# One graph network layer's edge pass, with a second job laid into it

## The chip, the cores and the metric

The program runs on one core of one Trainium2 chip. Its time is the device time of one execution in microseconds. The five engines that appear here are PE (TensorE, matrix products; its weight loads are listed apart as PEld), DVE (VectorE), ACT (ScalarE), POOL (GpSimd, which here issues the indirect DMAs that gather rows) and SP (SyncE, which issues the plain DMAs). Each engine has one queue and works it off in order. They meet only through semaphores.

## The reference, cut to what matters

Four graph layers follow one another over the same graph of 6250 nodes and 100,000 edges, each with a residual and a layer norm. The edges are sorted by their target `dst`, and the targets are dense at the start: `dst = 6250 * u**2`.

```python
edge_index = stack([src, dst])
x = layernorm(x + L0(x, node_vec1, src, dst, edge_attr_4, edge_attr_10, ...))
x = layernorm(x + L1(x, edge_index, ...))   # gated messages, GRU
x = layernorm(x + L2(x, edge_index, ...))   # two sort convolutions
x = layernorm(x + L3(x, edge_index, ...))   # four mean aggregations (SAGE)

def L0(...):                                # the tensor layer
    h = silu(edge_attr_10 @ W_fc1 / sqrt(10))      # edges x 100
    w = h @ W_fc2 / sqrt(100)                      # edges x 128
    x0s, x1s = y0[src], y1[src]                    # y = a linear map of the node's x
    ... = products of w, x0s, x1s and edge_attr_4
    agg = segment_sum(edge_features, dst)          # edges to 256 sums a node
def sage(z):                                # in L3
    mean = segment_sum(z[src], dst) / max(count, 1)
    return mean @ Wl.T + bl + z @ Wr.T
```

## The kernel before

**Edges and tiles.** A tile is 128 edges, one a partition; a group is four tiles; there are 196 groups. Nodes are columns: the 6250 nodes lie in 49 blocks of 128. Five regions of SBUF of 6400 columns (`X` and `A` to `E`, in the rows `x` and `ra` to `re`) hold node features and spare room.

**Two ways to sum over edges.** For a cold group POOL gathers the source rows of its edges by four indirect DMAs, and PE multiplies them with a one-hot matrix of the targets. For the first, hot part of the sorted edges, where many edges share few targets, the kernel builds once a count matrix: how many edges run from each source node to each of a range of target nodes. It lies in HBM as `dense`, in 16 bits, and the gate pass and the four SAGE passes read it back block by block and multiply it with the whole table of source rows; edges that it covers are not gathered there. The tensor layer (L0) has features of each edge's own and so gathers all 784 tiles.

**The count matrix.** Its target columns are cut in windows of `NARROW` = 32 nodes; a window takes as many whole tiles as fall into 27 expected nodes, 16 at most (`hot_cuts`, L51). For every tile DVE makes two one-hots, of the low seven bits of the source (128 wide, L1418) and of block and target together (49 x 32 = 1568 wide, L1419), PE multiplies them into PSUM (L1434), and ACT copies a finished window into a stage of eight windows (L1448), which SP stores to `dense`. 64 windows (380 tiles) are built in `build_phase`, which runs by itself before anything else of the network; the other 64 (148 tiles) are built inside the two sort phases of L2 by `LateBuild` (L2298, L2303, L2316, L2328), one tile at a turn between the sort's own instructions. The gate pass uses 2048 columns of it, the wide SAGE passes 2304, the slim ones 4096.

**The order of the phases.** Preparation of indices; build; scaling of weights; `table_phase`, which writes the table of `y` (L283, L299, L311); `tensor_pass`; its closing products; table, gate pass and GRU of L1; two sorts; then for each of the four SAGE layers a table, a pass and statistics. A phase is a block: all engines leave it before the next begins.

**The tensor pass** (L905 on) has for each group, by engine:
- POOL: four gathers (L953) into a ring of four groups of rows.
- SP: the next 10 x 512 edge inputs.
- PE: the hidden layer of the group after next as an f32 product over 10 rows (L996), the weights of the next group (four products, L1005), then 8 products with the one-hot of the targets (L1025, L1027).
- ACT: SiLU of the hidden layer (L970), four scaled copies of the gathered rows (L983).
- DVE: the one-hot of the targets (L1050), eight products and sums of the features (L852 to L864), two additions into the node regions (L1043).
The body is written once for four groups and looped 49 times. PE and DVE are one or two groups apart, held by semaphores; POOL may be four groups ahead.

**A SAGE pass** (`sage_pass`) lays 98 dense steps (49 blocks for each of two halves of the columns, three 16-bit terms of the table each, L1611) between its cold groups (products L1637), with the layer's own product (L1593). All steps lie in the cold groups but the last seven (wide) or five (slim). When a half is summed ACT copies it out of PSUM (L1568), DVE multiplies every window by its nodes' inverse counts (L1712) and adds it (L1720).

## Time and profile before

| | us |
|---|---|
| runs | 4872.65, 4879.16, 4879.4 |
| median | 4879.16 |
| the profiled execution | 4866.0 |
| its span on the core | 4863.8 |
| granted TensorE clock, mean | 0.873 |

The rows come from that one profiled execution. In it the preparation ends at 23.9 us, the build at 296, the first gather of the tensor pass starts at 325.2 and its last sums are added at 1358.5; the gate pass runs from 1448 to 2030, the sorts from 2175 to 2740, and the four SAGE passes from 2816, 3306, 3888 and 4450, of 364, 484, 483 and 347 us. A row of the stretches gives for each engine its busy time and in brackets its instructions. Busy times of PE are unions in which the tail of each product is modelled, so what a product costs is read from the distance of two starts. A row of a group of instructions gives count, busy time, mean duration in ns and the idle time before, with what ended it. Idle time of an engine that is not the bound costs nothing.

### The profile page before, as it was taken

How to read it: one execution, taken by the hardware profiler on the slowest of the kernel's cores; microseconds unless marked ns; L12 is line 12 of the kernel's file. 1: busy time of each engine (PE TensorE's matmuls, PEld its weight loads, DVE VectorE, ACT ScalarE, POOL GpSimd, SP SyncE). 2: the span in 40 equal slices, each digit the busy share in tenths (PEclk: the TensorE clock that was granted, in tenths of full speed). 3: DMA queues.
4: the chain of work that ended last, by engine and by line, in shares of the span. 5: the costliest groups of instructions: out<-in, count | busy, mean ns of one | idle time of the engine just before them, and what ended most of it. 6: DMA issues, size and time to landing. Idle time of an engine off the chain costs nothing. (4 is left out here: it accounts for less than half of the span.)

```text
span 4863.8 us, 78847 instructions
## 1 busy us (share of the span) xinstructions
PE 3902.5 (80%) x25115; PEld 2612.6 (54%) x25167; DVE 2854.8 (59%) x8895; ACT 1285.8 (26%) x2773; POOL 3033.0 (62%) x3029
## 2 busy tenths in 40 slices
PE   8978989888987777656645579968999599986995
PEld 3446667666664454433322345546767477664553
DVE  8966666666646767567768724263343634444234
ACT  1343333333324434343333400021011201012112
POOL 0037777777727767547757666727777477774764
PEclk9989898898889989876556789989999799997996
DMA  2352222222224434212243387818888388875873
GB/s 79 91 170 55 54 54 55 54 54 54 54 73 101 109 91 108 65 36 78 76 117 103 110 262 238 248 50 259 264 255 251 111 269 265 258 217 184 269 243 107
DMA packets 434350, 679.63 MB, mean 140 GB/s; under 512 B 66928, under 2 KB 297370, under 8 KB 433270
## 3 DMA queue, kind: packets, MB, share of 16 engines
q1 hardware_dynamic: 310774, 373.35, 24.5%
q0 software_dynamic: 123264, 302.38, 22.5%
q8 instruction: 164, 2.69, 0.2%
q14 instruction: 148, 1.21, 0.1%
HBM read 575.89 MB, written 99.58 MB: 139 GB/s over the span
## 5 line engine op out<-in xcount | busy, mean ns | idle before, releaser
L1541 POOL DMA_INDIRECT pass_rows<-table_sage,src_idx x1264 | 1231.0, 974 | 456.5 <-issue 368.4
L953 POOL DMA_INDIRECT pass_rows<-table_tensor,src_idx x784 | 783.3, 999 | 257.6 <-issue 236.8
L1672 DVE TENSOR_TENSOR pass_scaled_sums<-pass_sums_ps,rc 128x128 f32<-128x128 f32 x508 | 130.1, 287 | 955.4 <-PE pass_sums_ps L1637 949.8
L1611 PE MATMUL pass_dense_ps<-x 128*128 128x512 f16 (+3 forms) x3528 | 607.0, 327 | 31.8 <-DMA x<-table_sage 31.0
L1611 PE MATMUL pass_dense_ps<-rb 128*128 128x512 f16 x2352 | 535.2, 383 | 28.2 <-DMA rb<-table_sage 26.7
L1153 POOL DMA_INDIRECT pass_rows<-table_gate,src_idx x402 | 423.5, 1053 | 192.4 <-issue 116.4
L2375 POOL DMA_INDIRECT sort_rows<-table_sort,slot_idx x392 | 391.2, 998 | 183.1 <-issue 117.3
L1637 PE MATMUL pass_sums_ps<-pass_hot,pass_rows 128*128 128x128 bf16 x6096 | 412.0, 225 | 76.1 <-issue 74.4
L1611 PEld LDWEIGHTS pass_dense_ps<-x 128*128 128x128 bf16 x3528 | 314.4, 98 | 266.4 <-DMA x<-table_sage 32.4
L1025 PE MATMUL pass_sums_ps<-pass_hot,pass_prod_a 128*128 128x128 f32 x1568 | 363.1, 319 | 111.1 <-DVE pass_prod_b L852 110.9
L1637 PEld LDWEIGHTS pass_sums_ps<-pass_hot,pass_rows 128*128 128x128 bf16 x6096 | 383.6, 101 | 101.5 <-issue 83.1
L983 ACT ACTIVATE pass_y_ea<-pass_rows,rd 128x128 f32<-128x128 f32 x784 | 250.2, 390 | 507.1 <-DMA pass_rows<-table_tensor,src_idx 507.0
L1611 PEld LDWEIGHTS pass_dense_ps<-rb 128*128 128x128 bf16 x2352 | 226.9, 99 | 285.3 <-DMA rb<-table_sage 29.0
L1025 PEld LDWEIGHTS pass_sums_ps<-pass_hot,pass_prod_a 128*128 128x128 f32 x1568 | 284.0, 226 | 130.4 <-issue 129.8
L1027 PE MATMUL pass_sums_ps<-pass_hot,pass_prod_b 128*128 128x128 f32 x1568 | 354.0, 313 | 0.0
L2316 PE MATMUL sort_counts_ps<-sort_hot_key,sort_hot_low 128*128 128x512 bf16 (+1 forms) x571 | 193.2, 483 | 179.5 <-DVE sort_hot_key L2303 137.7
L1005 PEld LDWEIGHTS pass_weight_ps<-fc,pass_hidden 100*128 100x128 f32 x1576 | 201.2, 200 | 165.8 <-issue 162.7
L1238 PE MATMUL pass_dense_ps<-pass_weighted,rd 128*128 128x512 f32 x392 | 206.4, 651 | 102.2 <-DVE pass_weighted L1317 102.2
L1027 PEld LDWEIGHTS pass_sums_ps<-pass_hot,pass_prod_b 128*128 128x128 f32 x1568 | 287.8, 229 | 0.0
L1434 PE MATMUL build_counts_ps<-build_hot_key,build_hot_low 128*128 128x512 bf16 (+1 forms) x1490 | 266.4, 330 | 4.9 <-DVE build_hot_key L1419 2.6
L852 DVE TENSOR_TENSOR pass_y_ea<-pass_rows,rd 128x384 f32<-128x384 f32 x196 | 110.7, 565 | 240.4 <-DMA pass_rows<-table_tensor,src_idx 240.4
L996 PE MATMUL pass_hidden_ps<-pass_edge_in,fc 10*100 10x512 f32 x396 | 235.2, 675 | 18.3 <-DMA pass_edge_in<-in_edge_in 18.3
(331 smaller groups left out, 6758.6 us busy)
## 6 DMA issues: line engine op xcount, KB each, us to landing
rb<-dense SPq DMA_DIRECT2D x196, 512.0 KB, 3.8
x<-dense SPq DMA_DIRECT2D x196, 288.0 KB, 3.8
x<-table_sage SPq DMA_DIRECT2D x196, 192.0 KB, 4.7
pass_counts<-dense SPq DMA_DIRECT2D x98, 256.0 KB, 3.0
dense<-re SPq DMA_DIRECT2D x7, 3136.0 KB, 12.8
pass_rows<-table_sage,src_idx POOLq DMA_INDIRECT x1264
rb<-table_sage SPq DMA_DIRECT2D x196, 96.0 KB, 5.2
table_sage<-x SPq DMA_DIRECT2D x24, 768.0 KB, 3.5
```

What stands on the lines that cost most here:

```text
L953: nc.gpsimd.indirect_dma_start(rows[:, h, t, :], None, table, bass.IndirectOffsetOnAxis(ap=idx[:, at:at + 1], axis=0)).then_inc(gathered[h ...
L983: ins = nc.scalar.activation(y_ea0[:, r, t, :], rows[:, h, t, :], ACT.Copy, scale=cols(extra["edge_attr"], (q * GROUP_TILES + t) * 4, 1))
L996: nc.tensor.matmul(hidden_ps[0:HID, r4 % 2, :], extra["w_fc1"], edge_in[:, r4, :], start=True, stop=True).then_inc(hidden_summed, 1)
L1025: nc.tensor.matmul(sums[0][:, r, 0:WIN], prod_a[:, r, t, :], hot[:, r, t, :], start=first, stop=last)
L1027: ins = nc.tensor.matmul(sums[1][:, r, 0:WIN], prod_b[:, r, t, :], hot[:, r, t, :], start=first, stop=last)
L1153: nc.gpsimd.indirect_dma_start(rows[:, h, t, :], None, table, bass.IndirectOffsetOnAxis(ap=idx[:, at:at + 1], axis=0)).then_inc(gathered[h ...
L1238: ins = nc.tensor.matmul(dense_ps[:, at:at + 512], messages[:, k, 0:P], weighted[:, n % 2, at:at + 512], start=(b == 0), stop=(b == BLOCKS ...
L1434: ins = nc.tensor.matmul(counts[:, w % 2, at:at + wide], hot_low[:, r, :], hot_key[:, r, at:at + wide], start=(t == first), stop=(t == last))
L1541: nc.gpsimd.indirect_dma_start(rows[:, h, t, :], None, table, bass.IndirectOffsetOnAxis(ap=idx[:, at:at + 1], axis=0)).then_inc(gathered[h ...
L1611: ins = nc.tensor.matmul(dense_ps[:, at:to], table_ring[:, k, from_table:from_table + P], counts_ring[:, k, at - first:to - first], start= ...
L1637: ins = nc.tensor.matmul(sums[:, r, a * P:(a + 1) * P], rows[:, h, t, at:at + P], hot[:, r, t, :], start=(t == 0 and part == 0), stop=(t = ...
L2375: nc.gpsimd.indirect_dma_start(rows[:, b, j, :], None, table, bass.IndirectOffsetOnAxis(ap=slot_idx[:, at:at + 1], axis=0)).then_inc(gathe ...
```

## The change

**The build moves.** `build_phase` is gone. `tensor_pass` makes a `LateBuild` for the first 376 tiles and gives its turns to the first 190 of its 196 groups, two tiles a turn nearly everywhere: DVE makes the one-hots behind the group's own one-hot, PE multiplies behind the hidden layer, ACT copies a finished window behind its four row copies, and SP stores a finished stage. There is one stage (`E`), one PSUM accumulator for the window, and three buffers for the wide one-hot. The last SP work of the pass is the load of the node attributes, which before came ahead of the pass.

**The pass is written out.** All 49 turns of the loop are now separate code, on every engine.

**The first layer.** The 10 edge inputs and the 10 x 100 weights are each split in three bf16 terms; all nine pairs are stacked to 90 rows and one bf16 product (L1172 of the new program) takes the place of the f32 one. The edge inputs' terms are made in `first_table_phase`, eight chunks of 990 columns (ACT copy, DVE difference, POOL cast and DVE difference, then a store of 742 KB), beside the table; each store waits until the one before has landed. The pass reads them back in rounds of four groups, by three DMAs. The weights' terms are made in `split_weights` and go through HBM.

**Loads.** Weights, `x`, five of the eight chunks of edge inputs and the edge attributes are issued behind the preparation's own loads.

**The windows.** `hot_windows` chooses cuts and a width of its own for each window (at most 30 nodes wanted, some widened to 32) so that the widths just fill 1792, 2304 and 3840 columns. The gate pass reads 1792 columns (before 2048) for 376 tiles (380); the wide passes 2304 (2304) for 420 (404); the slim ones 3840 (4096) for 536 (528). With 784 tiles in all, cold groups are 102 (101), 91 (95) and 62 (64). A tile of the first 376 has 1232 key columns in the mean, at most 1470 (before 1568 each); in 41 of 68 places one window ends and the next begins in the same turn. The sorts build 160 tiles (148) of 1310 columns in the mean (1568).

**SAGE sums.** DVE copies the inverse counts of a half's windows side by side (`spread_counts`) and evacuates the half out of PSUM itself by one multiplication (`keep_dense`), so that a window then needs one addition. Before that ACT evacuated and DVE multiplied window by window.

```diff
@@ tensor_pass
-        sums = [s.ps(f"sums{a}", [P, 2, 512]) for a in range(A)]
+        sums = s.ps("sums", [P, 2, 512])
+        edge_terms = s.sb("edge_terms", [STACK, 2, ROUND_COLS], BF16)
+        build = LateBuild(nc, s, *extra["build"])
@@ sync
+            sp.wait_ge(extra["split_stored"], 16 * SPLIT)
+            stages = list(range(len(build.runs)))
+            for i in range(ITERS + 1):
+                if i >= 2:
+                    sp.wait_ge(hidden_summed, RING * (i - 1))
+                if i >= 1:
+                    sp.wait_ge(terms_loaded, 16 * PARTS * i)
...
+                for q in list(stages):
+                    if build.stage_turn(q, BUILD_TURNS) < RING * (i - 1):
+                        build.store(sp, stages.pop(0))
...
+            extra["attributes"].issue(sp)
@@ scalar, behind the four row copies
+                    for t in build.turns(q, BUILD_TURNS):
+                        for w in build.ended(t):
+                            build.evict(act, w)
-            looped(act, ITERS, body)
+            for i in range(ITERS):
+                body(i)
@@ tensor
-                nc.tensor.matmul(hidden_ps[0:HID, r4 % 2, :], extra["w_fc1"], edge_in[:, r4, :],
+                nc.tensor.matmul(hidden_ps[0:HID, :], extra["w_terms"],
+                                 edge_terms[:, q // RING % 2, q % RING * 512:(q % RING + 1) * 512],
...
-                    hidden_layer(i + (1 if h + LOOK >= 4 else 0), q + LOOK, r4)
                     weights(q + 1, (h + 1) % 2)
+                    hidden_layer(q + LOOK)
+                    for t in build.turns(q, BUILD_TURNS):
+                        build.products(pe, t)
@@ vector, behind the one-hot of the targets
+                for t in build.turns(q, BUILD_TURNS):
+                    build.one_hots(dve, t)
@@ LateBuild.evict
+        if w == first and stored > 0:
+            act.wait_ge(self.stored[q % n], 16 * stored)
+        act.wait_ge(self.counted, HOT_CUTS[w + 1] - self.start)
@@ sage_pass
-            def keep_dense(u):
-                if u > 0:
-                    act.wait_ge(dense_added, u * super_windows * A)
-                act.wait_ge(stepped, (u + 1) * BLOCKS)
-                nc.scalar.activation(kept, dense_ps[:, 0:sage_cols], ACT.Copy).then_inc(dense_kept, 1)
+            def keep_dense(u):
+                if u > 0:
+                    dve.wait_ge(dense_added, parts_of[u][0][0] * A)
+                dve.wait_ge(spread, sum(map(len, parts_of[:u + 1])))
+                dve.wait_ge(stepped, (u + 1) * BLOCKS)
+                for a in range(A):
+                    at = a * super_cols
+                    nc.vector.tensor_tensor(kept[:, at:at + super_cols], dense_ps[:, at:at + super_cols],
+                                            inv_dense[:, 0:super_cols], ALU.mult).then_inc(dense_kept, 1)
@@ gnn_kernel
-                build_phase(nc, "build", key, low, late_key[:], late_low[:], wide_iota, dense, [C, E], dense_stored,
-                            [first, attributes])
-            table_phase(nc, "tab0", [X], t0, ident, rhs=[wl1[:]], row_scale=attr_col, clear=[A[:], B[:]])
-            node_attributes.start_after(dense_stored, 16 * (GATE_WINDOWS // STAGE_WINDOWS))
+            first_table_phase(nc, X, t0, wl1[:], attr_col, [A[:], B[:]], [terms_out, terms_in], flat_edges, left, parts, flat_terms,
+                              edges_loaded, split_stored)
```

**The order on DVE** in the tensor pass, one group (turn) of the new program from one one-hot of the targets to the next. `rc` is room in region `C`: the 512 wide row makes the low one-hots of four tiles (every other turn), the x2 row the key one-hots of two tiles, here of windows 12 nodes wide.

```order
L1225 TENSOR_TENSOR pass_hot<-iota,rel 128x512 [waits prep_counted]
L2441 TENSOR_TENSOR rc<-rc 128x512 [waits pass0_counted]
L2447 TENSOR_SCALAR rc<-rc 128x588 [waits pass0_counted] x2
L1015 TENSOR_TENSOR pass_y_ea<-pass_rows,rd 128x384 [waits prep_step,gathered2]
L1015 TENSOR_TENSOR pass_w_y<-pass_weight_ps,pass_rows 128x128 [waits pass0_weight_made]
L1024 TENSOR_TENSOR pass_dot<-pass_y_ea 128x4x32 [waits pass0_step]
```

Before, the row after the one-hot of the targets was the product with the gathered rows; now three one-hot instructions of the build stand between them.

**The order on PE**, one group of the tensor pass, of the program before from one hidden layer to the next:

```order
L996 MATMUL pass_hidden_ps<-pass_edge_in,fc 100x512 [waits pass0_edge_in_loaded3,pass0_hidden_made]
L1003 REGISTER_ALU [waits prep_step]
L1005 MATMUL pass_weight_ps<-fc,pass_hidden 128x128 [waits pass0_hidden_made]
L1005 MATMUL pass_weight_ps<-fc,pass_hidden 128x128 x3
L1021 REGISTER_ALU
L1025 MATMUL pass_sums_ps<-pass_hot,pass_prod_a 128x128 [waits prep_step,prep_turned]
```

and the same stretch of the new one:

```order
L1182 MATMUL pass_weight_ps<-fc,pass_hidden 128x128 [waits pass0_hidden_made,prep_step]
L1182 MATMUL pass_weight_ps<-fc,pass_hidden 128x128 x3
L1172 MATMUL pass_hidden_ps<-pass_edge_terms,fc_stack 100x512 [waits pass0_hidden_made]
L2461 MATMUL pass_counts_ps<-rc 128x512 [waits pass0_key_made,pass0_low_made]
L2461 MATMUL pass_counts_ps<-rc 128x76
L2461 MATMUL pass_counts_ps<-rc 128x512 [waits pass0_key_made,pass0_low_made]
L2461 MATMUL pass_counts_ps<-rc 128x76
L1203 MATMUL pass_sums_ps<-pass_hot,pass_prod_a 128x128 [waits prep_step,prep_turned]
```

The hidden layer went behind the weights, and the products of two tiles of the count matrix stand ahead of the group's sums.

**The order on ACT** in the new tensor pass, around the end of a stage. `re` is the stage in region `E`:

```order
L2479 ACTIVATE re<-pass_counts_ps 128x49x26 [waits pass0_counted]
L1141 ACTIVATE pass_hidden<-pass_hidden_ps 100x512 [waits pass0_hidden_summed,pass0_weight_made]
L1154 ACTIVATE pass_y_ea<-pass_rows,rd 128x128 [waits gathered2,prep_step]
L1154 ACTIVATE pass_y_ea<-pass_rows,rd 128x128 x3
L2479 ACTIVATE re<-pass_counts_ps 128x49x20 [waits pass0_counted,dense_stored]
L1141 ACTIVATE pass_hidden<-pass_hidden_ps 100x512 [waits pass0_hidden_summed,pass0_weight_made]
```

Here the copies of windows stand between the SiLU and row copies of the groups, and the first copy of a new stage waits until the store of the one before has landed.

## Rows read from the trace of the kernel before

**Rows 1.** Stretches: us, busy (count) by engine; clock, DMA share, GB/s.

```profile
23.90:296.40 272.50, 266.39 (x1490) 119.70 (x1520) 266.92 (x762) 95.77 (x65) 0.00 (x0) 1.00 0.34 103
296.40:325.20 28.80, 15.51 (x98) 15.13 (x98) 8.72 (x14) 7.31 (x8) 10.80 (x2) 0.75 0.81 235
325.20:1358.50 1033.30, 911.55 (x5108) 697.09 (x5108) 704.16 (x2155) 357.68 (x982) 783.28 (x784) 0.87 0.22 57
...
2816.00:3180.00 364.00, 335.12 (x2195) 195.08 (x2194) 122.57 (x445) 21.53 (x51) 253.64 (x254) 0.96 0.79 245
3306.00:3790.00 484.00, 462.62 (x4364) 331.72 (x4364) 201.75 (x781) 46.69 (x100) 364.68 (x378) 0.98 0.82 255
...
4450.00:4797.00 347.00, 324.42 (x2093) 184.09 (x2094) 114.77 (x393) 45.72 (x99) 247.76 (x254) 0.96 0.81 249
```

**Rows 2.** DVE in order of time, in the build: start, duration, instruction.

```profile
149.98 0.62 DVE L1419 TENSOR_SCALAR build_hot_key<-wide_iota,key 128x1568 bf16<-128x1568 f16 x1
150.52 0.25 DVE L1418 TENSOR_SCALAR build_hot_low<-wide_iota,low 128x128 bf16<-128x128 f16 x1
```

**Rows 3.** Gathers on POOL: count, busy us, mean ns, idle before and its releasers.

```profile
L953 POOL DMA_INDIRECT pass_rows<-table_tensor,src_idx x784 | 783.3, 999 | 257.6 <-issue 236.8 <-POOLq L153 16.5 <-PE pass_sums_ps L1027 4.4
L1153 POOL DMA_INDIRECT pass_rows<-table_gate,src_idx x402 | 423.5, 1053 | 192.4 <-issue 116.4 <-POOLq L153 39.2 <-PE pass_sums_ps L1266 36.7
L2375 POOL DMA_INDIRECT sort_rows<-table_sort,slot_idx x392 | 391.2, 998 | 183.1 <-issue 117.3 <-POOLq L153 64.3 <-DVE sort_t L2444 1.5
```

**Rows 4.** One line's durations (ns min/median/max), first and last start.

```profile
L953 POOL DMA_INDIRECT pass_rows<-table_tensor,src_idx x784: 940/944/1536, 325.2 to 1348.8; - x196
```

**Rows 5.** DVE in order of time, one group of the tensor pass.

```profile
906.85 0.69 DVE L1050 TENSOR_TENSOR pass_hot<-iota,rel 128x512 f32<-128x512 f32 x1
908.55 0.56 DVE L852 TENSOR_TENSOR pass_y_ea<-pass_rows,rd 128x384 f32<-128x384 f32 x1 [1.01 <-DMA pass_rows<-table_tensor,src_idx]
...
909.90 0.29 DVE L852 TENSOR_TENSOR pass_prod_a<-pass_weight_ps,pass_y_ea 128x128 f32<-128x128 f32 x1 [0.40 <-ACT pass_y_ea L983]
...
911.84 0.69 DVE L1050 TENSOR_TENSOR pass_hot<-iota,rel 128x512 f32<-128x512 f32 x1
```

**Rows 6.** PE in order of time, tensor pass, at both clock levels.

```profile
907.88 0.39 PE L1027 MATMUL pass_sums_ps<-pass_hot,pass_prod_b 128*128 128x128 f32 x2
908.10 0.39 PE L1025 MATMUL pass_sums_ps<-pass_hot,pass_prod_a 128*128 128x128 f32 x2
...
908.64 1.10 PE L996 MATMUL pass_hidden_ps<-pass_edge_in,fc 10*100 10x512 f32 x2
909.67 1.16 PE L1005 MATMUL pass_weight_ps<-fc,pass_hidden 100*128 100x128 f32 x8
...
912.66 0.64 PE L1025 MATMUL pass_sums_ps<-pass_hot,pass_prod_a 128*128 128x128 f32 x2
913.09 0.63 PE L1027 MATMUL pass_sums_ps<-pass_hot,pass_prod_b 128*128 128x128 f32 x2
```

**Rows 7.** The wide one-hot inside the sort phases.

```profile
L2303 DVE TENSOR_SCALAR sort_hot_key<-keys_iota,late_key 128x1568 bf16<-128x1568 f16 x148 | 94.3, 637 | 0.0
```

**Rows 8.** Table phases: a PSUM evacuation on DVE, a cast on POOL.

```profile
L299 DVE TENSOR_TENSOR tab_rows<-tab_turned_ps,attr_col 128x896 f32<-128x896 f32 x7 | 7.6, 1092 | 14.4 <-DMA table_tensor<-tab_rows 7.6 <-PE tab_turned_ps L283 6.7
...
L351 POOL CAST x<-tab_rest 128x1024 bf16<-128x1024 f32 (+1 forms) x26 | 46.3, 1781 | 152.7 <-DVE tab_rest L400 152.5
```

**Rows 9.** DMA issues: count, KB each, median us from issue to landing.

```profile
dense<-re SPq DMA_DIRECT2D x7, 3136.0 KB, 12.8
...
table_sage<-x SPq DMA_DIRECT2D x24, 768.0 KB, 3.5
```

**Rows 10.** PE in order of time in a wide SAGE pass.

```profile
3450.25 1.50 PE L1637 MATMUL pass_sums_ps<-pass_hot,pass_rows 128*128 128x128 bf16 x24
3451.59 3.09 PE L1611 MATMUL pass_dense_ps<-x 128*128 128x512 f16 x18
3454.52 1.06 PE L1593 MATMUL pass_own_ps<-pass_z_block,sage_wr 128*128 128x128 f32 x8
```

610 lines of the change are left out of this document (374 added, 236 removed).

## The prediction

> **What bounds the kernel now.** I read the stretches first, to find the phases in which the change puts or takes work. From 23.9 to 296.4 us the build runs with DVE busy 267 of 272.5 us and PE 266, and POOL not at all [rows 1]. From 325.2 to 1358.5 the tensor pass has PE busy for 912 of 1033 us at a granted clock of 0.87, and DVE for only 704 [rows 1]. In the build, one key one-hot starts 0.54 us ahead of what follows it, though its duration is given as 0.62 [rows 2]: instructions overlap at their ends, so I cost DVE by distances of starts. Then the gathers: 784 of them have a mean of 999 ns and 236.8 us of "issue" between them, 0.302 us each, so 1.30 us for one and 5.2 us for a group of four; waits for PE are 4.4 us in all [rows 3]. First and last start are 325.2 and 1348.8, 1.307 us apart in the mean [rows 4]. POOL thus never rests: it sets the length of this pass. The group of DVE agrees. From one target one-hot to the next 4.99 us pass, and in them DVE is idle for 1.01 us until a gather lands and for 0.40 us until ACT has scaled the rows [rows 5]. It occupies 3.58 us of a group and leaves 1.4 to 1.6. On PE two starts of product pairs are 0.22 us apart at the full level (2.4 GHz) and 0.43 us at the lower one (1.2 GHz) [rows 6]. Eight pairs (1.78), the hidden layer (1.03, the distance to the next instruction) and the weights (about 1.0) make 3.8 us a group at the full level. A mean clock of 0.87 is 26% of the time at the lower level.
>
> **The tensor pass with the build in it.** A turn gets 376 / 190 = 1.98 tiles. DVE: a key one-hot has 1232 columns in the mean against 1568, between 0.42 us (in proportion to the 0.54) and 0.54; I take 0.45, since part of it does not shrink. The low one-hots of four tiles are one 512 wide instruction like the target one-hot, about 0.6, so 0.15 a tile. 1.98 x 0.60 = 1.2 us, and DVE is at 4.8 us of a group. That is less than POOL's 5.2, with 0.4 us to spare: the cover is thin but it is there. The added instructions stand where DVE now idles for the gather. PE loses the f32 hidden layer (1.03) and gets one product of 512 columns (0.22) and 1.98 x 1232 columns at 2.4 a ns (1.03): 4.0 us a group at full level. ACT has 358 us of work in the pass and gets 69 window copies of some 1.2 us; its time is no bound. Its place in the row matters: where one window ends and the next begins in one turn (41 times) PE waits about 1.5 us for the copy; PE has 1.2 us to spare a turn and the next turn makes up the rest, so I put it at nothing. Behind the wait for a stored stage ACT's SiLU and row copies queue, and PE and DVE behind these. A store lands 12.8 us after its issue, about 2.4 turns; the next stage's first window ends one to three turns after the old stage's last. So ACT is held for up to 8 us, at six places. POOL may be 16 gathers (21 us) ahead and DVE wins back 0.4 us a turn, with some 15 to 30 turns between the later stages: nothing in the sum, 48 us if none is made up.
>
> What isn't free is POOL against DVE. The median gather takes 944 ns, the mean 999 [rows 4, 3]: 55 ns each are lost already, in groups without a key one-hot. In the sort phases, where 148 key one-hots run beside 392 gathers, the mean is 998 [rows 7, 3], so the keys add nothing that can be told from the rest. If all the excess there (392 x 54 ns = 21 us) were the keys', one would cost 0.14 us. For 376 keys that bounds the price by 0 and 54 us; I take the middle, **+27 us**.
>
> The Trainium skill speaks against this part: "SBUF — State Buffer", section "Who interferes with whom", says that DVE in a two-port mode (16-bit `tensor_scalar` is of that kind) shuts GpSimd out of the shared port for the whole instruction, descriptor writing included. If every key one-hot did that, it would be the port rival below; the sort phases' mean of 998 ns does not bear it out.
>
> **The start.** The build goes with all its time; what it covered comes out. Its block covered the loads of `x` and the edge attributes, which now run behind the preparation's: `x` and five chunks of edge inputs are 5.6 MB, at the pace of a stage store (3136 KB in 12.8 us [rows 9]) 23 us after about 10, so 33 at the latest. The preparation is longer by two or three DVE instructions and a DMA (1.4 us by my estimate), then four key copies, waits and the scaling with the split of the weights (5 us). The table phase begins near 30 (26 to 34). The first chunk needs the ACT copy, DVE difference, POOL cast and DVE difference one after another behind a table evacuation. A DVE pass over 896 columns takes 1.09, a cast of 1024 on POOL 1.78 [rows 8]: 990 columns are about 1.2 and 1.7, and the first store is issued near 41. Then seven more. DVE has 1.09 + 2 x 1.2 = 3.5 us of work for each, and a store must land before the next is issued: one of 768 KB lands in 3.5 us [rows 9], with issue and handover 4.2. I take 4.2 (3.5 if DVE alone is the bound, 6.5 if table stores and reloads halve the pace). 41 + 7 x 4.2 = 70, and three block changes make 73 for the first gather (62 to 92), where it is at 325.2 now. **-252 us** (-263 to -233). That the first sums must wait until the terms are back, some 8 us, POOL's lead covers.
>
> **The other passes.** Gate: a step of 896 columns instead of 1024 is shorter by about 0.1 us on ACT and DVE and 0.2 on PE, 98 times, but only the 36.7 us in which POOL waits for PE [rows 3] can be won; one cold group more costs 4 x 1.4. **-3 us** (-15 to +8). Sorts: 160 tiles of 1310 columns for 148 of 1568, at the same POOL pace: nothing (+-4). Wide SAGE: a step is 2.93 us, the sums of a group 1.34, the own product of a block about 0.9 [rows 10]. While the steps last PE has 98 x 2.93 + 49 x 0.9 + 88 x 1.34 = 449 us against POOL's 88 x 4 x 1.25 = 440: both are full. The last seven groups are POOL's, 36 us. Sum 485, measured 484. Now there are 86 groups with steps and 5 without: 446 + 25.5 = 472. -13 each. Slim SAGE: PE is busy 335 of 364 and 324 of 347 us [rows 1]; a step loses 128 columns of three products, 0.16 us, 98 times, and eight tiles go with 24 products: 17 us if PE were the bound throughout, I take -14 each. Against that PE waits at each half for two multiplications of DVE (about 1.3 us each) behind whatever DVE is at, where it was one free ACT copy: +2 a pass (0 to +5). Together **-46 us** (-60 to -22).
>
> **The sum.** The profiled execution took 4866.0 us. -252 + 27 - 3 - 46 = -274 gives 4592. The median of the runs is 13.2 us above the profiled execution, and I carry that over: **4605 us**.
>
> **The rivals.**
> *DVE and ACT become the bound of the pass.* For it: DVE's 0.4 us a group. If the wait of 0.40 us for ACT stays and the one-hots cost their full durations (0.62 and 0.17), a turn is 3.58 + 0.40 + 1.98 x 0.79 = 5.54 against POOL's 5.33 with the contention of the sum: +40, and with 48 us of held ACT 4693. Against it: the waits are there because the gathers are late, and go when DVE is.
> *The port.* Each key one-hot stops a gather for its own 0.49 us (0.45 to 0.54): 376 x 0.49 = 184, 157 more than in the sum, 4762. Against it the 998 ns.
> *The saving is taken up by PE at the lower level: slower than before.* In place of the POOL bound PE bounds every turn. At 1.2 GHz a turn is 8.0 us, the pass 1568 us, 523 more than in the sum, 5130. For it: single accumulator waits break PE's work up, and PE is at the lower level 26% of the time now. It cancels the gain from a group of 6.7 us, 4.0 x (1 + s), so a share s of 0.68. Against it: a turn has more columns and less idle time than now, and the clock is 1.00 in the build, where PE is never idle [rows 1]. The skill's "TensorE: Matmul & The Clock Gate", section "What's actually happening", has it that activity releases the throttle, which would raise the clock here; the 0.87 and 1.00 agree.
> *The side gains don't come:* SAGE bound by its DMAs and chunks at 6.5 us: +46 and +16, 4667.
> *Better:* no contention, stage and table at their lower ends, 4550.
>
> **How the numbers follow.** Forecast 0.56 (4570 to 4640), DVE and ACT 0.18, port 0.05, lower level 0.02, side gains missing 0.12, better 0.07. The range leaves out the port, the lower level and the outer end of the others: 4545 to 4700. A measurement of this kernel can tell about 0.2% from no change; all cases but the lower level are faster by more. Faster 0.97, same 0.01, slower 0.02.
>
> **What would show it.** First gather at 62 to 92 us; a distance between gathers of 1.31 to 1.38 us over the pass with a mean near 1030 ns; POOL's waits for PE there still under 20 us; DVE busy near 90% and its wait for gathers much smaller; clock above 0.87; wide passes near 471, slim ones near 350 and 333. The forecast is wrong if gathers wait for PE's sums for tens of us, if many gathers last 1.4 us or more, or if the gate pass and the sorts move by over 10 us.

## The result, and the profile after

The changed kernel takes **4712.9 us** (median of four, 4711.0 to 4720.1) against 4879.3 for the kernel before (four, 4872.7 to 4879.7): a ratio of 0.9663, 95% interval 0.9649 to 0.9677. It is faster by 166 us, not by the 274 of the forecast (4605), and lies 13 us outside the range. The profiled execution took 4711.4 us, so between the two profiled executions the gain is 154.6 us (4866.0 less 4711.4), 120 less than the 274 of the sum. Between medians only 108 are missing. The 12 us between these two numbers are luck: the forecast carried over the 13.2 us by which the median stood above the profiled execution, and now that distance is 1.5.

The profile after, in stretches (us, then busy us and count by engine PE, PEld, DVE, ACT, POOL; clock, DMA share, GB/s): the first table phase, the tensor pass, the gate pass's two halves, the first slim SAGE pass, what follows it, a wide and the last slim pass.

```profile
30.00:94.80 64.80, 20.35 (x98) 19.10 (x98) 25.71 (x23) 16.14 (x17) 25.02 (x16) 0.63 0.52 165
94.80:1172.00 1077.20, 850.70 (x5879) 692.66 (x5880) 915.76 (x2598) 430.00 (x1041) 834.37 (x784) 0.93 0.33 90
1273.00:1576.00 303.00, 225.05 (x1281) 155.02 (x1281) 189.56 (x547) 118.23 (x296) 227.08 (x212) 0.89 0.39 99
1591.00:1870.00 279.00, 202.00 (x1160) 133.50 (x1157) 190.33 (x568) 113.93 (x294) 206.60 (x194) 0.93 0.38 94
2665.00:3025.00 360.00, 321.45 (x2156) 192.75 (x2156) 127.83 (x491) 17.62 (x48) 240.19 (x246) 0.94 0.76 237
3025.00:3166.00 141.00, 78.78 (x310) 56.05 (x310) 82.30 (x184) 31.81 (x44) 33.68 (x40) 0.78 0.19 70
3166.00:3630.00 464.00, 449.72 (x4236) 320.44 (x4236) 195.18 (x731) 42.44 (x97) 348.18 (x362) 0.99 0.82 258
4285.00:4630.00 345.00, 309.15 (x2060) 181.87 (x2060) 120.21 (x446) 41.62 (x96) 237.41 (x246) 0.95 0.77 239
```

Beside [rows 1]: the build's 272 us are gone; the tensor pass is 1077 us where it was 1024, at a clock of 0.93 for 0.87, with DVE at 85% and PE less busy than before; wide passes went from 482 to 463 us; slim ones stayed where they were (360 and 344 to 345) although they have 8 gathers less and 256 columns less.

The table sets the distances between gathers against the forecast, in us, all from profiled executions. The last column is e17, the best kernel of this study, explained below.

| stretch | before | after | change | forecast | e17 |
|---|---|---|---|---|---|
| to the first gather of the tensor pass | 325.2 | 94.8 | -230.4 | -252 | 81.1 |
| tensor pass, first gather to end of last | 1024.5 | 1076.9 | +52.4 | +27 | 1075.7 |
| to the gate pass's first gather | 98.8 | 101.4 | +2.6 | 0 | 103.2 |
| gate pass | 576.6 | 596.4 | +19.8 | -3 | 564.6 |
| to the end of the second sort | 705.5 | 712.1 | +6.5 | 0 | 706.8 |
| to the first SAGE gather | 85.5 | 83.9 | -1.6 | 0 | 83.9 |
| slim SAGE passes (two) | 703.9 | 703.6 | -0.3 | -24 | 674.2 |
| wide SAGE passes (two) | 962.0 | 927.1 | -34.8 | -22 | 925.2 |
| between and after the SAGE passes | 381.9 | 413.4 | +31.5 | 0 | 349.8 |

The gathers answer to [rows 3] (busy us, mean ns, idle before them and what ended it):

```profile
L1124 POOL DMA_INDIRECT pass_rows<-table_tensor,src_idx x784 | 834.4, 1064 | 246.8 <-issue 236.8 <-PE pass_sums_ps L1203 5.7 <-POOLq L201 4.3
L1333 POOL DMA_INDIRECT pass_rows<-table_gate,src_idx x406 | 433.7, 1068 | 202.3 <-issue 118.2 <-PE pass_sums_ps L1452 44.5 <-POOLq L201 39.6
```

POOL still sets the pass: 236.8 us of issue as before and 5.7 us of waits for PE. A gather is 65 ns longer, and 784 x 65 ns = 51 us is the whole of the pass's +52. So the missing 120 us are: the start 22, the contention of this pass 25, the gate pass with the gap ahead of it 25, the sorts with the gap ahead of them 7, and SAGE 41, most of that between the passes and not in them.

**What the queues show.** The stretches that follow a slim pass are longer by 11 us each, and PE waits there for DVE (once for 13.0 us). DVE's row in order of time, at the end of the last pass (in brackets its idle time before and what ended it):

```profile
4628.16 7.49 DVE L1847 TENSOR_TENSOR ra<-ra,pass_kept 128x32 f32 x24 [5.20 <-issue]
...
4642.50 7.45 DVE L1847 TENSOR_TENSOR ra<-ra,pass_kept 128x24 f32 x24 [5.18 <-issue]
```

and at the start of the same pass, with the same number of windows:

```profile
4305.13 2.81 DVE L1821 COPY pass_inv_dense<-rc 128x28 f32 x24 [1.41 <-issue]
```

5.2 us of "issue" against 1.4 ahead of 24 windows. What stands there is the load of 24 window starts into registers. It is listed on the sequencer (DVEq, PEldq), with the least, median and longest duration in ns, then first and last start. Before:

```profile
L1123 DVEq TENSOR_LOAD <-bases x50: 309/355/979, 1475.4 to 2041.9; - x50
L1123 PEldq TENSOR_LOAD <-bases x26: 306/336/348, 1458.5 to 2033.1; - x26
...
L1646 DVEq TENSOR_LOAD <-hot_bases x40: 818/1104/1415, 2993.3 to 4813.5; - x40
```

After:

```profile
L1303 DVEq TENSOR_LOAD <-bases x51: 315/961/982, 1300.4 to 1889.0; - x51
L1303 PEldq TENSOR_LOAD <-bases x26: 530/1004/1026, 1284.4 to 1871.5; - x26
...
L1760 DVEq TENSOR_LOAD <-hot_bases x64: 310/1604/5383, 2686.4 to 4665.7; - x64
```

Put beside the first table entry that each load asks for (worked out from the window and group counts of both kernels), the loads of these passes fall into two rows, PE and DVE within 0.1 us of each other; only the first load of the first slim pass stands out, with 3.3 us:

```
values loaded                       4      6      8     12     16     24
first entry a multiple of 4      0.34   0.82   0.60   0.85   1.10   1.60 us
any other first entry            0.97   1.41   1.85   2.73      -   5.37 us
```

The change moved first entries. The second half of a slim pass began at window 64 and begins at 73; of a wide one at 36, now 45; the starts of the gate pass's cold groups were read from entry 96 on, now from 95. (The kernel before had such loads too: sixes from entries that are no multiple of 4 in its wide passes, 1.41 us, and fours in the gate and SAGE passes, 0.97.)

### The profile page after: what moved, and what is told of

It reads as the page before. It is cut to its first block and busy times, and to the rows that moved or that the text cites. A ratio compares the mean times of both kernels' runs of the same rounds, so it can differ in the third digit from the quotient of the medians.

```text
span 4709.5 us, 73302 instructions
## 1 busy us (share of the span) xinstructions
PE 3546.9 (75%) x24179; PEld 2502.4 (53%) x24180; DVE 2819.4 (60%) x8637; ACT 1252.7 (27%) x2796; POOL 3057.2 (65%) x2999
## 5 line engine op out<-in xcount | busy, mean ns | idle before, releaser
L1664 POOL DMA_INDIRECT pass_rows<-table_sage,src_idx x1216 | 1175.8, 967 | 476.7 <-issue 350.3
L1124 POOL DMA_INDIRECT pass_rows<-table_tensor,src_idx x784 | 834.4, 1064 | 246.8 <-issue 236.8
L1725 PE MATMUL pass_dense_ps<-rb 128*128 128x512 f16 (+1 forms) x2352 | 508.7, 373 | 27.4 <-DMA rb<-table_sage 25.2
L2461 PE MATMUL sort_counts_ps<-sort_hot_key,sort_hot_low 128*128 128x512 bf16 (+4 forms) x502 | 190.8, 519 | 194.2 <-DVE sort_hot_key L2447 150.5
L1203 PE MATMUL pass_sums_ps<-pass_hot,pass_prod_a 128*128 128x128 f32 x1568 | 234.9, 297 | 131.8 <-DVE pass_prod_b L1015 131.0
L1203 PEld LDWEIGHTS pass_sums_ps<-pass_hot,pass_prod_a 128*128 128x128 f32 x1568 | 209.7, 206 | 186.7 <-issue 177.8
L2461 PE MATMUL pass_counts_ps<-rc 128*128 128x512 bf16 (+8 forms) x1039 | 238.1, 355 | 88.5 <-ACT re L2479 88.5
L1424 PE MATMUL pass_dense_ps<-pass_weighted,rd 128*128 128x512 f32 (+1 forms) x392 | 191.8, 616 | 113.2 <-DVE pass_weighted L1503 110.7
L1203 PE MATMUL pass_sums_ps<-pass_hot,pass_prod_b 128*128 128x128 f32 x1568 | 228.9, 294 | 0.0
L1182 PE MATMUL pass_weight_ps<-fc,pass_hidden 100*128 100x128 f32 x1576 | 221.5, 286 | 1.5 <-ACT pass_hidden L1141 1.0
L1203 PEld LDWEIGHTS pass_sums_ps<-pass_hot,pass_prod_b 128*128 128x128 f32 x1568 | 212.8, 211 | 0.0
```

What stands on the lines that cost most here:

```text
L1124: nc.gpsimd.indirect_dma_start(rows[:, h, t, :], None, table, bass.IndirectOffsetOnAxis(ap=idx[:, at:at + 1], axis=0)).then_inc(gathered[h ...
L1182: ins = nc.tensor.matmul(weight_ps[:, r, t * P:(t + 1) * P], hidden[:, r, t * P:(t + 1) * P], extra["w_fc2"], start=True, stop=True)
L1203: ins = nc.tensor.matmul(sums[:, r, a * WIN:(a + 1) * WIN], prod[:, r, t, :], hot[:, r, t, :], start=(t == 0), stop=(t == GROUP_TILES - 1))
L1424: ins = nc.tensor.matmul(dense_ps[:, at:to], messages[:, k, 0:P], weighted[:, n % 2, at:to], start=(b == 0), stop=(b == BLOCKS - 1))
L1664: nc.gpsimd.indirect_dma_start(rows[:, h, t, :], None, table, bass.IndirectOffsetOnAxis(ap=idx[:, at:at + 1], axis=0)).then_inc(gathered[h ...
L1725: ins = nc.tensor.matmul(dense_ps[:, at:to], table_ring[:, k, from_table:from_table + P], counts_ring[:, k, at - first:to - first], start= ...
```

## The experiments

The register loads, the split's order on DVE, the one-hots and the transfers were each tried alone. e5 to e16 form a second group: there the kernel before takes 5498 to 5500 us and not 4878 to 4881 as beside the others. The record numbers the chips 12, 14 and 1 in this group and 13 and 14 in the first, so the number of the chip does not tell them apart; what does is not known. What is compared in the second group is compared with runs of that group. There is no result of e4, in which each key one-hot was to be written twice.

**e1: register loads from a multiple of four.** In both `load_bases` of the gate and SAGE passes:

```diff
+lead = at % 4
-source[0:1, at:at + count]
+source[0:1, at - lead:at + count]
-return values
+return values[lead:]
```

> The changed kernel, with one edit: each batched load of window starts into registers (gate pass on TensorE and VectorE, SAGE passes on VectorE) begins at a table entry whose number is a multiple of 4, with up to three entries more than are used. Theory A: in the changed kernel such a load costs about 0.22 us for each value when it begins elsewhere (24 values 5.37 us, 12 values 2.73 us, 8 values 1.85 to 1.93 us, 4 values 0.96 to 1.0 us), and 1.60, 0.85, 0.60 and 0.34 us when it begins at a multiple of 4; the change moved the second half's windows from 64 or 36 to 73 and 45, and the gate pass's cold groups from 95 to 94, off such entries. Then the loads of 24 fall to about 1.8 us, the gate pass (596 us from first to last gather) gets 10 to 18 us shorter, its gap between the halves 4 us, each slim SAGE pass and its tail 15 to 22 us, each wide one 5 to 8 us: 55 to 85 us in all, about 4630 to 4660 us. Theory B: the loads lie beside waits, and the passes are longer because the adds of 24 windows are one chain: then the loads get shorter but the time falls by less than 15 us, to no less than 4698 us.

Measured: 4653.0 us, ratio 0.9536 (0.9512 to 0.9559), 60 us off. Its profiled execution was its fastest, 4636.5, so its stretches add up to 75 us of gain where the medians have 60. The slim passes took 347.2 and 331.5 us (360 and 344), what follows the first slim one 131.0 (141.2), the tail 69.9 (80.3); wide passes with their gaps were 7.0 and 8.6 us shorter; the gap between the gate's halves was 11.1 us for 16.2. DVE ahead of the same 24 windows:

```profile
4570.89 7.43 DVE L1849 TENSOR_TENSOR ra<-ra,pass_kept 128x24 f32 x24 [1.67 <-issue]
```

Theory A. With this alone the slim passes are 13 and 12 us below those of before, which is the forecast's term. Only the gate pass was short of it, 9 us of 10 to 18 (587.5 us; in four profiles with the loads as they were, of after, e2, e3 and e18, it took 595.0 to 609.0, so these 9 are hardly more than the scatter). The expectation names entries 95 and 94; they are 96 and 95, and 94 and 95 are both no multiples of 4, so nothing else in it changes. On PE a load was no faster than before the edit, since 4 values had become 7.

```profile
L1304 PEldq TENSOR_LOAD <-bases x26: 593/1064/1082, 1284.6 to 1858.5; - x26
```

**e2: the third term ahead of the next remainder.** In the first table phase on DVE:

```diff
+                if 0 <= i - 1 < SPLIT:
+                    third_term(i - 1)
                 if i < SPLIT:
                     take_first(i)
-                if 0 <= i - 1 < SPLIT:
-                    third_term(i - 1)
```

> The changed kernel, with two calls exchanged on VectorE in the first table phase: the third term of chunk i-1 is made before the first remainder of chunk i. Theory A: a chunk takes 8 us there, not 4.2, because the store of chunk i-1 stands behind the remainder of chunk i, which waits for ScalarE's copy, which waits for the landing of the store of chunk i-2: landing (4.5 us), copy, remainder and third term in one chain. With the exchange the store of chunk i-1 no longer waits for that landing, the pace falls to 5 to 6 us a chunk, and the first gather of the tensor pass moves from 94.8 to 72 to 82 us; the time falls by as much, to 4690 to 4700 us. Theory B: the pace is set by the stores themselves (landing after landing, with the table's store and a reload between them on the same queue), and stays at 7 to 8 us; the first gather stays within 5 us of 94.8.

Measured: 4700.6 us, ratio 0.9623 (0.9600 to 0.9647), 12 us off; first gather at 80.3, 14.5 us sooner. The profiled execution was the slowest of its four, 4713.2, with a gate pass of 609.0 us; no edit touches that pass. One chunk in after, from the landing of a store (ACT's copy, then DVE's remainder, then its third term of the chunk before) to the next store's issue:

```profile
45.69 1.03 ACT L393 ACTIVATE re<-re 128x990 bf16<-128x990 f32 x1 [8.94 <-DMA edge_terms<-re]
...
46.75 1.19 DVE L430 TENSOR_TENSOR re<-re 128x990 f32<-128x990 f32 x1 [4.54 <-ACT re L393]
...
47.86 1.18 DVE L435 TENSOR_TENSOR re<-re 128x990 bf16<-128x990 f32 x1
48.01 1.90 POOL L383 CAST re<-re 128x990 bf16<-128x990 f32 x1 [4.55 <-DVE re L430]
49.07 0.36 SPq L460 DMA_DIRECT2D edge_terms<-re  x1
```

and issues of stores in order of time, after:

```profile
41.24 0.38 SPq L460 DMA_DIRECT2D edge_terms<-re  x1
...
49.07 0.36 SPq L460 DMA_DIRECT2D edge_terms<-re  x1
...
57.16 0.36 SPq L460 DMA_DIRECT2D edge_terms<-re  x1
```

and in e2:

```profile
52.23 0.36 SPq L460 DMA_DIRECT2D edge_terms<-re  x1
...
58.00 0.36 SPq L460 DMA_DIRECT2D edge_terms<-re  x1
...
63.79 0.36 SPq L460 DMA_DIRECT2D edge_terms<-re  x1
```

8.0 us a chunk became 5.8: theory A. A store lands 4.2 us after its issue (median; 3.8 in e2), and in after 3.4 us of copy, remainder and third term follow before the next one. The exchange also parted POOL's casts from DVE's third term; of after and of e2 (busy us, mean ns, idle before):

```profile
L383 POOL CAST re<-re 128x990 bf16<-128x990 f32 x6 | 10.3, 1718 | 55.2 <-DVE re L430 55.2
```

```profile
L383 POOL CAST re<-re 128x990 bf16<-128x990 f32 x6 | 6.1, 1010 | 51.0 <-DVE re L430 51.0
```

The first mean mixes durations: of all eight casts six run beside a third term (L435) from nearly their start to its end and take 1.90 us, one takes 1.70 and one 1.01; in e2 none overlaps a third term and all take 1.01.

**e3, e18: the one-hots of the build left out.** Key one-hots 8 columns wide after the first three tiles (e3), and the low ones 8 of 128 too after two groups (e18):

```diff
+some = keys
+if self.start == 0:
+    some = BUILD_KEYS if t < self.RINGS else 8
-self.nc.vector.tensor_scalar(self.hot_key[:, r, 0:keys], self.iota[:, 0:keys], ...
+self.nc.vector.tensor_scalar(self.hot_key[:, r, 0:some], self.iota[:, 0:some], ...
```

> The changed kernel, where the wide key one-hots of the tensor pass's build are written for the first three tiles only and 8 columns wide after that, so that the matrix of counts is wrong; products, evictions, stores and all waits stay. Theory A: a gather takes 1064 ns in the tensor pass instead of 999 because VectorE's 16-bit key one-hots (376 of 561 ns) hold up GpSimd; without them the mean is 995 to 1010 ns, and the pass from first to last gather takes 1020 to 1035 us instead of 1077. Theory B: the gathers are held up by the added transfers (the stacked terms three times over, the seven stores of the matrix): the mean stays above 1045 ns and the pass above 1060 us.

> The kernel of e16_no_hots (key and low one-hots of the tensor pass's build 8 columns wide; the matrix of counts is wrong), which beside the unaltered one took 28 ns off the mean gather, and e14_no_low_hots 10 ns, where the gathers had waits of their own. Where they have none, e3_no_key_hots took off 38 ns of 65. Theory A (the rest is the low one-hots and scales as the key one-hots do): another 12 to 25 ns, a mean of 1001 to 1014 ns and a pass of 1025 to 1042 us. Theory B (the rest is not the one-hots'): 1018 to 1026 ns and 1044 to 1050 us.

Measured, in e3 and in e18 (one execution of each):

```profile
L1124 POOL DMA_INDIRECT pass_rows<-table_tensor,src_idx x784 | 804.4, 1026 | 249.7 <-issue 235.9 <-PE pass_sums_ps L1203 9.5 <-POOLq L201 4.3
```

```profile
L1124 POOL DMA_INDIRECT pass_rows<-table_tensor,src_idx x784 | 783.9, 1000 | 255.5 <-issue 236.5 <-PE pass_sums_ps L1203 14.8 <-POOLq L201 4.2
```

The mean goes 1064, 1026, 1000, and before it was 999 [rows 3]; the pass 1077, 1050, 1035 us. So e3 fell between its theories, and e18 confirms the first: the one-hots are all of it. The key ones cost 38 ns a gather, 30 us in all or 0.08 us for each of 376; the low ones 26 ns, 20 us or 0.22 us for each of 94. The last 10 us between 1035 and the 1024.5 of before are POOL's waits for the sums, 14.8 us against 4.4. The added transfers are all there in e18, whose gather is as long as before: they have no part in the mean.

**e7, e11, e14, e16, e8, e12: the same question in the second group.** e7, e11 and e16 are e18's kernel, e14 has the low one-hots alone 8 wide, e8 and e12 (one kernel) load the stacked terms in full for two rounds only, and 8 columns after that:

```diff
+wide = wide if i < 2 else 8
```

> As e3_no_key_hots, and the low one-hots of the tensor pass's build are written 8 columns wide too after the first two groups (the matrix of counts is wrong). e3_no_key_hots took the mean gather from 1064 to 1026 ns, not to 999. Theory A: the other 27 ns are VectorE's as well, the low one-hots (94 of 681 ns) and the small instructions: the mean falls to 1000 to 1015 ns. Theory B: they are the added transfers: the mean stays at 1020 to 1030 ns.

> The changed kernel where the stacked edge terms are loaded in full for the first two rounds of the tensor pass only, and 8 columns wide for the other 47 (the first layer's result is wrong). Theory A: added transfers are part of what lengthens the gathers: the mean falls from 1064 to 1040 to 1050 ns and the pass from 1077 to 1055 to 1065 us. Theory B (VectorE alone): the mean stays at 1058 to 1068 ns, the pass within 5 us of 1077.

> The kernel of e7_no_hots again (key and low one-hots of the tensor pass's build written 8 columns wide; the matrix of counts is wrong), for a look beside e3_no_key_hots where the gathers have no other waits. In e7_no_hots the mean gather fell from 1041 (e5_whole_fours there) to 1004 ns. Theory A (VectorE's one-hots are the whole of it): 995 to 1012 ns, and the pass 1022 to 1038 us. Theory B (the low one-hots have no part): 1020 to 1030 ns as in e3_no_key_hots, and the pass 1045 to 1055 us.

> The kernel of e8_less_traffic again (the stacked terms in full for two rounds of the tensor pass only; the first layer's result is wrong), for a look where the gathers have no other waits. In e8_less_traffic the mean was 1044 ns beside 1041 in e5_whole_fours. Theory A (transfers have a part): mean 1040 to 1050 ns, pass 1055 to 1065 us. Theory B: mean 1058 to 1068 ns, pass 1072 to 1082 us.

> The changed kernel with only the low one-hots of the tensor pass's build written 8 columns wide after the first two groups (94 instructions of 681 ns become short; the matrix of counts is wrong). e3_no_key_hots took 38 of the 65 ns that a gather gained. Theory A (the other 27 ns are the low one-hots): the mean falls by 20 to 30 ns against e13_changed_again, the pass by 15 to 22 us. Theory B (they come from the instructions' number and what shifts against what, not from these): by less than 10 ns and 8 us.

> The kernel of e7_no_hots and e11_no_hots beside the unaltered one: key and low one-hots both 8 columns wide (the matrix of counts is wrong). Theory A (VectorE's one-hots are the whole of what a gather gained): its mean is 55 to 65 ns under e13_changed_again's where nothing else holds the gathers, and the pass 45 to 55 us shorter; where the gathers wait for remote, 30 to 40 ns and 10 us or less. Theory B (27 ns are not theirs): 35 to 42 ns and 25 to 32 us.

Mean gather there: 1032 ns in the changed kernel (e13), 1033 to 1041 in five others with all one-hots, 1004, 1010 and 1005 without any, 1023 without the low ones, 1044 and 1034 with fewer transfers. Transfers have no part that shows; the low one-hots have some 10 ns, the key ones some 18. The pass lengths say little: 1220 to 1234 us without one-hots and 1248 in e13, but 1231 to 1237 in e5, e8 and e12, which have them all, since gathers have a wait of their own there. Several expectations were written for the 1064 ns of the first group and can't be held against these runs: e8's 1044 ns fits its theory A and e12's 1034 neither, yet both are what the unaltered kernel has there, and e11 met its mean but not its pass. Of those with a yardstick of the group e14 missed both theory A's 20 ns and theory B's 8 us (9 ns, 13.5 us), and e16 fell short of A's 30 ns (27). e18 gave the clean number.

**e13: the changed kernel in the second group.**

> The changed kernel itself, unaltered, as the yardstick for the runs beside it: e5 to e12 ran where the kernel before takes 5498 us and the gathers have a wait of their own (releaser remote) in every fourth or fifth, and there was no run of the changed kernel there. Every theory expects 4712 us and the stretches already read if the kernel before takes 4878 us here. If the kernel before takes about 5498 us, theory A (the register loads' cost is the same there, 50 to 80 us over all passes) expects 5285 to 5315 us, e5_whole_fours having taken 5234; theory B (it is hidden there behind the remote waits) 5240 to 5265 us.

Measured: 5291.3 us, ratio 0.9611 (0.9591 to 0.9631). POOL in order of time in a wide SAGE pass:

```profile
3705.85 0.95 POOL L1664 DMA_INDIRECT pass_rows<-table_sage,src_idx  x1 [0.30 <-issue]
3708.15 0.95 POOL L1664 DMA_INDIRECT pass_rows<-table_sage,src_idx  x1 [1.35 <-remote]
```

The gather itself takes 0.95 us as elsewhere, but in the wide passes about every fourth starts 1 us late (552 us for 463), with "remote" as its releaser or a DMA of an earlier phase; in the tensor pass 69 of 784 have "remote". Theory A for the loads: e5, below, is 58 us under it.

**e5, e10, e15, e17: whole fours, then the three repairs together.** e5 ends each load at a multiple of four as well; e10 adds e2; e15 and e17 (one kernel) also halve the slim passes' parts:

```diff
+source[0:1, at - lead:min(at + count + -(at + count) % 4, source.shape[1])]
...
-24 if A == 1 else 12
+12 if A == 1 else 12
```

> The changed kernel with every batched load of window starts beginning at a multiple of 4 table entries, as in e1_aligned, and also ending at one (up to three more entries behind, not used). Theory A: a batched load fetches four values at a time only where a whole four lies in it, and the others one by one at 0.22 to 0.24 us: e1_aligned's loads of 7 (TensorE 1.06 us, VectorE 0.82 us) go to about 0.6 us, those of 25 to 28 values stay at about 1.8 us or fall to it. The gate pass has four such loads per 4 groups on its two chained engines, so it gets 5 to 15 us shorter than in e1_aligned (first half 302 us, second 274), the SAGE passes 0 to 5 us each; the time is 4625 to 4645 us, against 4653 for e1_aligned. Theory B: the gate pass's added time is not in these loads: its halves stay at 300 to 304 and 272 to 276 us, and the time is within 8 us of e1_aligned's.

> e5_whole_fours and e2_swap together: the 16-bit first layer stays, its splitting runs at 5.8 us a chunk, and the register loads are in whole fours. If the two repairs lie in different stretches and add up (theory A): first gather at 80 us, gate halves of 296 to 300 and 268 to 274 us, and 4625 to 4640 us where the kernel before takes 4878 (12 us below e1_aligned's 4653 for the start, and up to 12 for the gate pass). Theory B (what the start gains is given back in the gate pass, as the profile of e2_swap had it, with 287 us in the second half): the time is within 8 us of e1_aligned's.

> e10_swap_whole_fours with the slim SAGE passes' windows spread and added 12 in a part instead of 24 (7 parts of each half instead of 4, so that the dense steps end three groups sooner). With whole-four loads a part of 24 still takes VectorE 9 to 10 us where a group of gathers takes 5, and the three groups at the half's end stand at 7.8, 14.1 and 9.7 us. Theory A (VectorE's part is what makes these groups long): with 12 they are 5 to 7 us, and each slim pass with its tail gets 5 to 12 us shorter: 10 to 25 us under e10's ratio of 0.9488. Theory B (TensorE's dense steps bind, and they have now 54 instead of 57 groups): no gain, within 5 us of it, the groups at the half's end shorter and all others longer.

> e15_parts_of_12 unaltered. Its ratio to the kernel before was 0.9428 where that took 5500 us. Where the kernel before takes 4878 us and the gathers have no wait of their own, theory A (register loads, split order and part size all cost what they showed, and add up: 60, 12 and some 15 us off 4713) expects 4610 to 4635 us, and the gate pass's second half at 268 to 275 us; theory B (the gate pass is slower for another reason than register loads) the same time within 10 us of 4640, with the gate's halves at 300 and 275 or more.

Measured in the second group: e5 5233.7 us (ratio 0.9506), e10 5214.2 (0.9488), e15 5184.1 (0.9428, 0.9409 to 0.9448), where e13 took 5291.3. In the first group: **e17 4567.1 us, ratio 0.9361 (0.9340 to 0.9381)**, better than both kernels and 43 us below the lowest time that a theory gave it. Its loads of the gate pass on PE, its gate pass, and its last pass with the tail:

```profile
L1304 PEldq TENSOR_LOAD <-bases x26: 587/590/832, 1271.3 to 1820.9; - x26
```

```profile
1260.00:1825.00 565.00, 422.88 (x2506) 286.41 (x2506) 386.70 (x1134) 238.28 (x604) 423.49 (x406) 0.94 0.37 100
...
4179.00:4507.00 328.00, 304.60 (x2060) 180.50 (x2060) 129.06 (x491) 41.61 (x95) 240.39 (x246) 0.95 0.79 251
4507.00:4564.00 57.00, 20.14 (x105) 16.23 (x105) 28.45 (x153) 20.56 (x58) 14.44 (x7) 0.50 0.19 59
```

The gate pass is 564.6 us, 32 under after and 12 under before. POOL's waits for PE in it are 20.9 us for 44.5, and its mean gather is 1043 ns for 1068. The longest break between two of its gathers is 5.0 us, for 16.2 in after and 11.6 before. e19, below, has the same loads without the exchange, and its gate pass takes 567.5 us; both lie far under the 595.0 to 609.0 of the four profiles with the loads as they were. In the second group the same edit does not show in this pass (633.6, 638.3 and 642.8 us in e5, e10 and e15 for 639.4 in e13), where gathers have the wait of their own. Part size: at the first half's end three groups of gathers took 7.8, 14.1 and 9.7 us in e1 and 6.2 each in e17; e15 is 30 us under e10. I did not run whole fours alone in the first group, so what they and the smaller parts give there is not told apart, save in the gate pass, which has no such parts.

**e6, e9, e19: the 16-bit first layer undone.** The edge inputs are loaded as fp32, no splitting; e9 with e5's loads, e19 with all of e17's but the exchange, which has no place there.

```diff
-edge_terms = s.sb("edge_terms", [STACK, 2, ROUND_COLS], BF16)
+edge_terms = s.sb("edge_terms", [BASIS, 2, HALF])
...
-nc.tensor.matmul(hidden_ps[0:HID, :], extra["w_terms"], ...
+nc.tensor.matmul(hidden_ps[0:HID, :], extra["w_fc1"], ...
```

> The changed kernel with the 16-bit first layer undone: the edge inputs are loaded as fp32 into 10 rows (1024 columns at a time) and multiplied with the fp32 weights of the first layer; the splitting of the edge inputs in the first table phase, its stores and its reloads are gone. The build stays in the tensor pass. Theory A: the pass is bound by the gathers, with TensorE at 851 us busy of 1077; the fp32 product costs TensorE about 0.55 us more a group (108 us in all), which it has, so the pass stays at 1060 to 1090 us, while the first gather comes at 60 to 72 us instead of 94.8: 25 to 35 us less in all, about 4680 to 4690 us. Theory B: TensorE's chain of a group is what holds back the buffers of the gathers once the build's products are there too; then the pass is 30 to 100 us longer, POOL shows waits for the sums, and the time is 4710 to 4780 us.

> e5_whole_fours and e6_fp32_first_layer together: register loads in whole fours, and the fp32 first layer in the tensor pass with no splitting at the start. Where e6_fp32_first_layer ran, the kernel before took 5497.65 us, and the gathers of every kernel waited 1.3 us more in every fourth or fifth of them (releaser shown as remote); there the first gather came at 53.7 us instead of 93, and the pass took 1260 us against 1236 for e5_whole_fours. Theory A (the gathers bound the pass, and TensorE has room for 0.78 us more a group): where the kernel before takes about 4878 us, the pass takes 1075 to 1095 us, the first gather comes at 54, and the time is 4590 to 4615 us. Theory B (TensorE's chain binds with the fp32 product): the pass takes 1110 us or more and the time is 4630 to 4680 us, above e10_swap_whole_fours.

> e17_parts_of_12 with the fp32 first layer of e6_fp32_first_layer instead of the 16-bit one and its splitting. The fp32 product took 0.78 us more a group (two passes of 0.67 us against one of 0.39), the first gather came at 54 us instead of 80. Where the gathers had waits of their own, the pass got 50 us longer than in e10_swap_whole_fours (1273 against 1223) and the whole 30 us. Theory A (the pass is bound by the gathers where they have no such waits): the pass takes 1075 to 1095 us, the first gather comes 26 us sooner, and this kernel is 10 to 25 us below e17. Theory B (TensorE's chain binds with the fp32 product on any chip): the pass takes 1105 us or more and the kernel is slower than e17 by 5 to 40 us.

Measured: e6 5277.1 us (0.9602), 14 under e13, and e9 5244.2 (0.9551), 30 over e10, both with intervals that overlap those of their partners; e19 4594.3 (0.9419, 0.9399 to 0.9440), 27 over e17 and clear of it. Its first gather comes at 54.7, 26 us sooner, and its pass takes 1118.5 us, 43 more:

```profile
L1149 PE MATMUL pass_hidden_ps<-pass_edge_terms,fc 10*100 10x512 f32 x392 | 217.7, 635 | 11.7 <-DMA pass_edge_terms<-in_edge_in 11.0 <-ACT pass_hidden L1119 0.7
...
L1102 POOL DMA_INDIRECT pass_rows<-table_tensor,src_idx x784 | 836.0, 1066 | 297.0 <-issue 231.7 <-PE pass_sums_ps L1180 50.7 <-POOLq L201 14.6
```

Theory B: with PE at 973 of 1096 us busy the gathers wait 50.7 us for sums. The 16-bit layer earns 43 us in the pass and costs 26 at the start in e17's order. In the changed kernel's own order the start costs 40 (first gather at 94.8 for 54.7). By these numbers next to nothing would be left there, but that pair was not run in the first group; in the second e6 was 14 us faster, within the intervals.

## Why the prediction was wrong, point by point

- **What bounds the pass: right.** POOL, with 5.7 us of waits for PE where "under 20" was asked, 1.374 us from gather to gather (1.31 to 1.38), DVE's wait for gathers down from 240 to 92 us (for ACT only from 71 to 62), the clock up at 0.93 (above 0.87). DVE's 85% is less than "near 90%". ACT waited for stores four times, 21.1 us in all (up to 9.6), and POOL's waits for PE stayed at 5.7, so holding ACT cost nothing that shows. The rivals on DVE and ACT, on the lower clock and on the port fall.
- **Contention: mechanism right, one term left out.** The mean gather is 1064 ns and not "near 1030". +27 was meant for the key one-hots, and they cost 30; that the middle of 0 and 54 came so close is luck, no row had picked it. The low ones, priced as DVE time (0.15 us a tile) and not as contention, cost another 20. The bounds of 0 and 54 held the sum, but the upper one was read off a phase in which low one-hots run too, so "keys" was the wrong name for it. The Trainium skill, "SBUF — State Buffer", section "Who interferes with whom", says a two-port `tensor_scalar` shuts GpSimd out for the whole instruction. By the trace's mean of 0.56 us a key one-hot that would be up to 0.56 us each (my estimate), and 0.08 was measured. The same section infers that a `tensor_tensor` does not hold up descriptor writing, where the low one-hots, of that kind, cost 0.22 us each. Its rule that a DVE instruction with two SBUF inputs holds up a GpSimd instruction that reads SBUF agrees with the casts, 1.90 us beside the third term and 1.01 without.
- **The start: the failed step is "I take 4.2"**, a store's landing with issue and handover as the pace of a chunk. The prologue was right to a fraction of a microsecond (first store issued at 41.24, forecast 41), and so was the landing, 4.2 us after issue. But two buffers and DVE's order put copy, remainder and third term behind each landing: 7.4 to 8.4 us from store to store but for the last, beyond the 6.5 of the upper end, and 5.8 when that order is exchanged (e2). So the first gather came at 94.8, outside the 62 to 92. Order on an in-order engine was read from the diff as work per chunk, not as a chain of who waits for whom.
- **Slim SAGE and the stretches behind the passes: the failed step is one that isn't there.** "Two multiplications of DVE, +2 a pass" was the only price for the second half; the loads of 24 starts stood in no sum, they were taken at nothing without a reason. Each slim pass has six of them in its second half, three before the windows are spread and three before they are added, 3.8 us more each: 23 us, of which 12 lengthened the pass and ate its -12, and 10 the stretch behind it (e1: slim passes 13 and 12 under before, as forecast, and the stretches back at 131 and 70). The rival "side gains don't come" had nearly the size, 46 us for 41, with the wrong cause.
- **Wide SAGE: right in its way, short in its size**, -18.1 and -16.7 for -11 each, at 463 us where "near 471" was asked; why it gained more was not followed; its loads of 12 (2.73 us) cost the 4 and 6 us in the stretches behind.
- **Gate: the failed step is the -3 itself, a sum of columns and one more group** in which the reading of the starts stood at nothing. The pass took 19.8 us more, and over 10 was the prediction's own sign of being wrong. Moving the boundary by one group took one load for every four groups from 0.34 to about 1 us on PE and one on DVE, and at the half's end PE's loads of 8 from 0.59 to 1.93; with whole fours the pass is 32 us shorter (e17), and its waits fall with them. It is then 12 under before, inside the forecast's -15 to +8.
- **Sorts: +6.5 us for nothing, with the gaps around them.** The two phases went from 252.7 and 257.4 to 257.4 and 258.1 us with 12 tiles more to build, beyond the +-4 by a little, and stay there in e17 (257.4 and 261.7). Not followed further.

The range failed because the start, the contention and the side gains all came out near or beyond their upper ends (+22, +25 and +41 for +16, +27 and +46, which is 4694 by themselves), and the gate's 25 us and the sorts' 7 came on top; 12 came back by the luck of the carried 13.2. With the starts of the loads alone mended (e1, 4653) the time lies inside it; with the order and the parts too (e17) it is 38 us below the forecast.

## What to carry to other kernels

When a change moves a boundary (a first group, a first window), look at every table that is read from that boundary: a batched register load is one line in the code and up to 5 us on its engine, and the profile lists it only on the sequencer, as idle "issue" time of the engine. For a pipeline through several in-order engines, write the chain of one round with its waits before pricing it by the slowest part; two buffers overlap little if a consumer stands behind the next producer on its own engine. And price what is added beside POOL's gathers by all the 16-bit instructions it brings, not by the widest.

## What the runs showed of the hardware

A load of several values from SBUF into registers takes about 0.25 us for each four when it begins at a multiple of four entries (16 bytes), and 0.22 to 0.25 us for every value otherwise: 24 values take 1.60 or 5.37 us on DVE, 8 take 0.59 or 1.93 on PE. Left-over values behind the last whole four are single too (7 values 1.06 us on PE, 8 values 0.59). The Trainium skill, "Runtime: NRT & Kernel Launch", section "Instruction fetch mechanics", gives about 200 ns a register "even for bulk" (of loads from HBM); the loads here agree with it only where they begin elsewhere than at a whole four.

One kernel took 4879 us beside some runs and 5500 us beside others, 12.7% more, and chip number 14 stands in both groups. A gather lasts the same (967 and 972 ns in the changed kernel's SAGE passes) and the clock is nearly the same (0.858 and 0.840), but many gathers start about 1 us late, every fourth or so in the wide passes. What they wait for, and what sets the two groups apart, stays open.
